# Early stage of a graph network kernel: centring of x shared by ScalarE and POOL, turning over two banks, and four smaller moves

## The reference

```python
h = relu(layernorm(x))
# self loops are added to edge_index once more inside; deg counts both
dinv = rsqrt(segment_sum(1, dst));  norm = dinv[src] * dinv[dst]
conv(h, W, b) = segment_sum((h @ W)[src] * norm, dst) + b
x1 = x + conv(relu(conv(relu(conv(h, W1, b1)), W2, b2)), W3, b3)
h = relu(layernorm(x1))
red = segment_sum(h[src] + relvectors[edge_type], dst)
out = x1 + gru_cell(red, h)
```

## Time and profile before

| | us |
|---|---|
| median of 3 runs (range) | 964.29 (962.75 to 965.47) |
| the profiled execution, whole | 963.61 |
| its span | 959.3 |
| PE busy | 913.2 (95%) |
| DVE busy | 480.2 (50%) |
| ACT busy | 291.5 (30%) |
| POOL busy | 18.7 (2%) |

### The profile page before, as it was taken

The page is one execution under the profiler, slowest core; times in us unless marked ns, Lnnn a source line. Parts: engine busy times, 40 slices in busy tenths (PEclk is TensorE's granted clock), DMA queues, the critical chain, the costliest instruction groups (busy, mean ns, idle before and its releaser), DMA issues.

```text
span 959.3 us, 15812 instructions
## 1 busy us (share of the span) xinstructions
PE 913.2 (95%) x6300; PEld 567.1 (59%) x6300; DVE 480.2 (50%) x1266; ACT 291.5 (30%) x569; POOL 18.7 (2%) x29
## 2 busy tenths in 40 slices
PE   2879999999999989999999999999999999999996
PEld 1358788888888875544445544444455455555553
DVE  7956889899988810211114233333535033333436
ACT  3565455555555520100112022111332121212222
POOL 0000100000000000000000000000000000000000
PEclk9979999999999999999999999999999999999999
DMA  6000000000000040000000011111321000100010
GB/s 210 5 1 1 3 12 18 13 13 13 13 13 13 13 160 1 2 1 1 0 1 11 29 34 44 39 34 39 97 74 30 8 22 23 33 23 22 23 33 30
DMA packets 27350, 27.65 MB, mean 29 GB/s; under 512 B 3217, under 2 KB 25901, under 8 KB 27272
## 3 DMA queue, kind: packets, MB, share of 16 engines
q1 hardware_dynamic: 26600, 26.18, 8.7%
q10 hardware_dynamic: 672, 0.41, 0.1%
HBM read 17.43 MB, written 9.15 MB: 28 GB/s over the span
## 4 chain that ended last, share of the span: by engine, by line
PE 91%; DVE 5%; ACT 2%; issue 1%; DMA 0%; SPq 0%; ACTq 0%; DVEq 0%
PE ps L1079 41%; PE ps L789 12%; PE ps L697 11%; PE ps L549 9%; PE ps L1090 5%; PE ps L553 5%; PE ps L1110 2%; PE ps L769 2%; DVE node_b L798 1%; PE ps L702 1%; PE ps L713 1%; PE ps L756 1%; PE ps L737 1%; PE ps L534 1%; PE ps L711 0%
## 5 line engine op out<-in xcount | busy, mean ns | idle before, releaser
L1079 PE MATMUL ps<-count,node_b 128*128 128x512 f16 (+3 forms) x1400 | 271.2, 352 | 0.4 <-DVE node_b L1241 0.3
L798 DVE TENSOR_TENSOR node_b<-node_b 128x50 f16<-128x50 f16 (+4 forms) x455 | 209.3, 526 | 10.6 <-PE ps L697 9.9
L1079 PEld LDWEIGHTS ps<-count,node_b 128*128 128x128 f16 (+2 forms) x1400 | 121.4, 97 | 142.4 <-issue 8.2
L697 PE MATMUL ps<-node_b 128*128 128x225 f16 (+1 forms) x808 | 165.8, 288 | 9.4 <-DVE node_b L798 9.4
L1000 ACT ACTIVATE count<-ps 128x500 f32 x202 | 122.8, 608 | 127.2 <-PE ps L697 120.9
L789 PE MATMUL ps<-node_a,count 128*128 128x256 f16 (+1 forms) x1050 | 149.1, 273 | 0.0
L1079 PE MATMUL ps<-count,node_a 128*128 128x512 f16 (+3 forms) x700 | 135.4, 352 | 0.0
L789 PEld LDWEIGHTS ps<-node_a,count 128*128 128x128 f16 (+1 forms) x1050 | 100.0, 98 | 21.6 <-issue 7.6
L1079 PEld LDWEIGHTS ps<-count,node_a 128*128 128x128 f16 (+1 forms) x700 | 60.0, 97 | 74.1 <-issue 7.2
L702 PE MATMUL ps<-node_b,params 128*128 128x9 f16 (+1 forms) x808 | 101.4, 174 | 0.0
L697 PEld LDWEIGHTS ps<-node_b 128*128 128x128 f16 x808 | 81.3, 101 | 17.8 <-DVE node_b L798 7.1
(11 more groups left out here) (196 smaller groups left out, 809.5 us busy)
## 6 DMA issues: line engine op xcount, KB each, us to landing
node_a<-in_x SPq DMA_DIRECT2D x4, 768.0 KB, 7.6
table_scratch<-agg SPq DMA_DIRECT2D x21, 128.0 KB, 1.7
node_b<-table_scratch SPq DMA_DIRECT2D x3, 768.0 KB, 6.8
xt<-x_scratch SPq DMA_DIRECT2D x16, 128.0 KB, 2.1
out<-scaled SPq DMA_DIRECT2D x16, 128.0 KB, 1.7
xt<-in_x SPq DMA_DIRECT2D x12, 128.0 KB, 2.1
params<-in_x SPq DMA_DIRECT2D x12, 128.0 KB, 2.0
x_scratch<-xt SPq DMA_DIRECT2D x12, 128.0 KB, 1.7
```

The source lines that it names most:

```text
L697: return PE.matmul(window(s)[:, :, first:first + n], low, key_hot[k][j // 2][:, j % 2, :, i].rearrange("p (t w) -> p t w", w=n), start=(s ...
L798: return DVE.tensor_tensor(to, iota, keys.unsqueeze(2).to_broadcast([P, n, width, 2]), ALU.is_equal)
L1079: last = PE.matmul(ps[:, b, 0:cols], nodes[0:k, t, part, f * P:(f + 1) * P], count[0:k, t, c * CHUNK:c * CHUNK + cols], start=(n == 0 and ...
```

## The change

- The root's table: ACT takes one small square root at the start of its program, ahead of the loads of the edge types.
- Centring: ACT centres the even tiles in their beats, POOL the odd ones at the start of `fast_pool`, as soon as the sums are there.
- Turning: tiles 0 to 8 use bank 6 as before; from tile 9 on, tiles alternate between banks 6 and 7, and PE waits for the relu of the tile before the last.
- Ranks' counts: both halves go into bank 5, as rows 0 to 19 and 32 to 51 of one sum; ACT copies them out in one instruction, and four matmuls turn them in place of eight. The moving operand of L737 is now pairs out of every four, and `both_ranks`, made by DVE in beat 0, adds the two sets of rows.
- `COLUMNS`: PE's beat 25 becomes beat 7; DVE's maximum moves from beat 33 to beat 16, and the steps for the scales become six.
- The end of the build: 24 of the 1050 early products are kept for the last block. What is left to do for tiles 19 and 20 on DVE and ACT comes behind the last loops and the last window; SP stores these two within the reload of the last group.

```diff
-        picks, counts_t = aside(4, 2 * WINDOW - 1), aside(5, EACH)
+
+        COUNT_ROWS = 32 + WINDOW
+        picks, counts_t = aside(4, 2 * COUNT_ROWS - 1), aside(5, EACH // 2).rearrange("p (s j) -> p s j", j=2)
+        both_ranks = aside(4, WINDOW, 2 * COUNT_ROWS)
...
+            ACTE.activation(scales[:, 7:8], asked[:, 0, 0:1], ACT.Sqrt).then_inc(*act_seq.up())
             load_rows(ACTE, rel_row, rel, types_in)
...
-        SCALE_STEPS = 7
+        SCALE_STEPS = 6
...
-        COLUMNS_AT = 25
+        COLUMNS_AT = 7
+        COLUMNS_OUT_AT = 16
+        LATER_TURNS = 8
...
-        products_after = [-(-max(s + 1 - PRODUCTS_FROM, 0) * len(early_products) // (NS - PRODUCTS_FROM)) for s in range(NS)]
-        assert products_after[-1] == len(early_products)
+
+        LAST_PRODUCTS = 24
+        products_after = [-(-max(s + 1 - PRODUCTS_FROM, 0) * (len(early_products) - LAST_PRODUCTS) // (NS - PRODUCTS_FROM)) for s in range(NS)]
+        products_after[-1] = len(early_products)
...
-        counts_bank = (5, 7)
-        CNT, HIST, TURNED = ps[:, 5, 0:WINDOW * Q], ps[:, 5, WINDOW * Q:WINDOW * Q + T], ps[:, 6, 0:D].rearrange("p (f n) -> p f n", f=HALVES)
+        RANKS = ps[0:COUNT_ROWS, 5, 0:EACH // 2].rearrange("p (s j) -> p s j", j=2)
+        CNT, HIST = ps[:, 5, 0:WINDOW * Q], ps[:, 5, WINDOW * Q:WINDOW * Q + T]
+
+        def turned(t):
+            bank = 6 if t <= LATER_TURNS else 6 + t % 2
+            return ps[:, bank, 0:D].rearrange("p (f n) -> p f n", f=HALVES)
...
                 PE.wait_ge(ranks_ready, beat + 2)
-                for h, bank in enumerate(counts_bank):
-                    last = PE.matmul(ps[0:WINDOW, bank, 0:EACH // 2], picks[:, WINDOW - 1 - beat:2 * WINDOW - 1 - beat],
-                                     rank_is[beat][:, h * EACH // 2:(h + 1) * EACH // 2], start=(beat == 0), stop=(beat == WINDOW - 1))
+                ranks = rank_is[beat].rearrange("p (s j) -> p s j", j=QUARTERS)
+                for h in range(2):
+                    row = 32 * h + beat
+                    last = PE.matmul(RANKS, picks[:, COUNT_ROWS - 1 - row:2 * COUNT_ROWS - 1 - row], ranks[:, :, 2 * h:2 * h + 2],
+                                     start=(beat == 0 and h == 0), stop=(beat == WINDOW - 1 and h == 1))
                 if beat == WINDOW - 1:
                     last.then_inc(ranks_counted, 1)
             if beat == COUNTS_AT:
-                PE.wait_ge(counts_out, 2)
+                PE.wait_ge(counts_out, 1)
                 for q in range(Q):
-                    for j in range(QUARTERS):
-                        last = PE.matmul(CNT[0:lanes(q), q * WINDOW:(q + 1) * WINDOW],
-                                         counts_t[0:WINDOW, :].rearrange("p (s j) -> p s j", j=QUARTERS)[:, q * P:q * P + lanes(q), j],
-                                         ident16[0:WINDOW, 0:WINDOW], start=(j == 0), stop=(j == QUARTERS - 1))
+                    for j in range(2):
+                        last = PE.matmul(CNT[0:lanes(q), q * WINDOW:(q + 1) * WINDOW], counts_t[0:COUNT_ROWS, q * P:q * P + lanes(q), j],
+                                         both_ranks[0:COUNT_ROWS, :], start=(j == 0), stop=(j == 1))
                 last.then_inc(counts_done, 1)
             t = beat - TURN_AT
             if 0 <= t < T:
                 m = rows(t)
-                PE.wait_ge(x_centred, t + 1)
+                PE.wait_ge(x_centred[t % 2], t // 2 + 1)
+                if t == LATER_TURNS + 1:
+                    PE.wait_ge(columns_read, 1)
                 if t:
-                    PE.wait_ge(x_turned_out, t)
+                    PE.wait_ge(x_turned_out, t if t <= LATER_TURNS else t - 1)
                 for f in range(HALVES):
-                    last = PE.transpose(TURNED[:, f, 0:m], h1[0:m, t, f * P:(f + 1) * P], ident[0:m, 0:m])
+                    last = PE.transpose(turned(t)[:, f, 0:m], h1[0:m, t, f * P:(f + 1) * P], ident[0:m, 0:m])
                 last.then_inc(x_turned, 1)
...
-                    PE.wait_ge(columns_read, 1)
...
             if beat == COLUMNS_AT:
                 PE.wait_ge(abs_made, 2)
-                PE.wait_ge(counts_out, 2)
...
-                        if s == min(summed_at[u] + OUT_AT, NS - 1):
+                        if s == summed_at[u] + OUT_AT:
                             out_bias_dve(u)
-                        if s == min(summed_at[u] + OUT_LOW_AT, NS - 1):
+                        if s == summed_at[u] + OUT_LOW_AT:
                             out_low_dve(u)
             DVE.wait_ge(win_written, NS)
             loops(ALU.add, EARLY).then_inc(chunk_looped, 1)
+            for u in range(EARLY):
+                if summed_at[u] + OUT_AT >= NS:
+                    out_bias_dve(u)
+                if summed_at[u] + OUT_LOW_AT >= NS:
+                    out_low_dve(u)
 
         def beside_dve(beat):
 
             if beat == 0:
                 DVE.memset(picks, 0.0).then_inc(*dve_seq.up())
                 DVE.wait_ge(*dve_seq.now)
-                DVE.memset(picks[:, WINDOW - 1:WINDOW], 1.0).then_inc(ranks_ready, 1)
+                DVE.tensor_tensor(both_ranks, ident16[:, 0:WINDOW], ident16[:, 32:32 + WINDOW], ALU.add).then_inc(*dve_seq.up())
...
+            if beat == COLUMNS_OUT_AT:
+                columns_max_dve()
...
+        def columns_max_dve():
+            DVE.wait_ge(abs_summed, 1)
+            DVE.tensor_reduce(fours[:, 0:2], COLUMNS, AX_X, ALU.max).then_inc(columns_read, 1)
...
             if step == 0:
-                DVE.wait_ge(abs_summed, 1)
-                DVE.tensor_reduce(fours[:, 0:2], COLUMNS, AX_X, ALU.max).then_inc(columns_read, 1)
-            elif step == 1:
...
-                    if s == min(summed_at[u] + OUT_AT, NS - 1):
+                    if s == summed_at[u] + OUT_AT:
                         out_shape_act(u)
+            for u in range(EARLY):
+                if summed_at[u] + OUT_AT >= NS:
+                    out_shape_act(u)
...
+            if 0 <= t < T and t % 2 == 0:
                 m = rows(t)
                 ACTE.wait_ge(x_summed, min(t // 6, XG) + 1)
-                ACTE.activation(h1[0:m, t, :], h1[0:m, t, :], ACT.Identity, bias=moments[0:m, t, 0:1], scale=2.0).then_inc(x_centred, 1)
+                ACTE.activation(h1[0:m, t, :], h1[0:m, t, :], ACT.Identity, bias=moments[0:m, t, 0:1], scale=2.0).then_inc(x_centred[0], 1)
             t = beat - TURN_AT
             if 0 <= t < T:
                 m = rows(t)
                 ACTE.wait_ge(x_turned, t + 1)
-                ACTE.activation(turned_x(t)[:, :, 0:m], TURNED[:, :, 0:m], ACT.Relu).then_inc(x_turned_out, 1)
+                ACTE.activation(turned_x(t)[:, :, 0:m], turned(t)[:, :, 0:m], ACT.Relu).then_inc(x_turned_out, 1)
             if beat == WINDOW - 2:
                 ACTE.wait_ge(ranks_counted, 1)
-                for h, bank in enumerate(counts_bank):
-                    ACTE.activation(counts_t[0:WINDOW, h * EACH // 2:(h + 1) * EACH // 2], ps[0:WINDOW, bank, 0:EACH // 2],
-                                    ACT.Copy).then_inc(counts_out, 1)
+                ACTE.activation(counts_t[0:COUNT_ROWS, :, :], RANKS, ACT.Copy).then_inc(counts_out, 1)
...
-            for u in range(EARLY):
+            def store(u):
                 SP.wait_ge(node_ready, u + 1)
                 SP.dma_start(early_dram(u, u + 1)[:, 0, :], staged[u % 2].rearrange("p a d -> p (a d)")).then_inc(early_stored[u % 2], 16)
+
+            stored = next(u for u in range(EARLY) if summed_at[u] + OUT_LOW_AT >= NS)
+            for u in range(stored):
+                store(u)
             SP.wait_ge(win_done, NS)
             SP.wait_ge(win_written, NS)
-            for k in range(2):
-                SP.wait_ge(early_stored[k], 16 * len(range(k, EARLY, 2)))
             for g, (first, end) in enumerate(RELOADS):
+                for u in range(stored, end):
+                    store(u)
+                stored = max(stored, end)
+                for k in range(2):
+                    SP.wait_ge(early_stored[k], 16 * len(range(k, end, 2)))
                 SP.dma_start(node_b[:, first:end, :, :].rearrange("p t a d -> p t (a d)"), early_dram(first, end)).then_inc(early_in[g], 16)
...
         def fast_pool():
+            for t in range(1, T, 2):
+                m = rows(t)
+                POOL.wait_ge(x_summed, min(t // 6, XG) + 1)
+                POOL.tensor_scalar(h1[0:m, t, :], h1[0:m, t, :], 2.0, moments[0:m, t, 0:1], ALU.mult, ALU.add).then_inc(x_centred[1], 1)
             POOL.wait_ge(small_maxed, 2)
......
```

More of the change, by code:

```diff
@@ L597, in program @@
         w_early_in, bias1_in, small_in = [sem(f"w_early_in{i}") for i in range(2)], sem("bias1_in"), sem("small_in")
-        x_centred, x_turned, x_turned_out, x_weighted = (sem(n) for n in ("x_centred", "x_turned", "x_turned_out", "x_weighted"))
+        x_turned, x_turned_out, x_weighted = (sem(n) for n in ("x_turned", "x_turned_out", "x_weighted"))
+        x_centred = [sem(f"x_centred{i}") for i in range(2)]
```

(15 more changed lines are left out.)

## The result

| | before | after |
|---|---|---|
| median, us (range) | 964.41 (962.75 to 965.47, 4 runs) | 955.34 (953.45 to 956.55, 4 runs) |
| the profiled execution, whole | 963.61 | 956.55 |
| its span | 959.3 | 952.4 |

The changed kernel takes 0.9906 of the time, 95% interval 0.9882 to 0.9929: 9.1 us less, where the forecast had 6.6. The profiled execution is the longest of the four.

What follows compares the result with a forecast made beforehand. PE was taken as the bound from 100 to 338 us, so gains could come only between 20 and 100 us and at the 338 us gap. 4.2 + 2.35 = 6.6 us off gave 957.7 us, range 953.5 to 964.0.

Steps and rivals of the forecast that it cites:

- (g): End of the build: 46 products behind the last window remove PE's 2.43 us wait before L1110, 2.35 net.
- Root's table: ACT's early table load delays the edge types' issue by 1.5 us against slack of 3.4: no effect.
- (a): DVE before window 2: 0.1 us for `both_ranks`, three collisions with POOL at 0.23 each; window 2 0.8 us later.
- (b): Columns' sums in PE's beat 7: 2.3 us, bounds 1.65 and 3.3; PE 3.1 us late by then.
- (c): Tiles 0 to 11: 0.5 us saved on tiles 9 to 11, another 0.7 in rounds; window 6 at 49.5.
- (d): Tiles 12 to 15: ACT sets the pace, 2.9 us; window 7 at 52.4, DVE begins L897 at 53.4.
- (e): From L897 to window 8: DVE needs 1.25 and 2.05 us; window 8 at 56.8, 3.5 us ahead.
- (f): Window 8 to the degrees: 0.7 us saved, bounds 0 and 1.5; 4.2 us ahead at the first early product.
- clock stays up: Rival: denser work keeps PE at 2.4 GHz up to 100 us, giving 955.0 us; chance 0.15.
- Port: Rival: DVE and POOL share their way to memory; 12 centrings cost DVE 10.1 us, giving 964.1; chance 0.18.
- Slow centring: Rival: POOL too slow for its 12 tiles; at 4 us each the kernel takes 973.3 us; chance 0.07.

Runs made afterwards that it cites:

- after_again: The changed kernel once more, nothing altered: 956.11 us, 0.9916 of the kernel before.
- front_only: The changed kernel without the part at the end of the build: 959.55 us, 0.9948 of the kernel before.
- cols_3_warm: Changed kernel with columns in beat 3, maxima in 10, two banks throughout, POOL centring odd tiles to 17, tiles 19 and 24's transposes repeated: 951.57 us.
- end_only: The kernel before with only the end's part, 24 early products kept for the last block: 961.63 us, 0.9971 of the kernel before.
- all_pool: The changed kernel with all 25 tiles centred by POOL, none by ACT: 955.07 us, 0.9902 of the kernel before.
- act_all: The changed kernel with all 25 tiles centred by ACT, none by POOL: 955.28 us, 0.9907 of the kernel before.

## Why the prediction was right

The measured 955.34 lies within the range of 953.5 to 964.0, 2.4 us below the forecast of 957.7: the steps are right, and their sum is too small. Its own steps against the profile after.

| step | forecast | profile after |
|---|---|---|
| window 6 | 49.5 | 49.87 |
| window 7 | 52.4 | 52.54 |
| DVE begins L897 (now L919) | 53.4 | 53.67 |
| window 8 | 56.8 | 57.06 |
| degrees' first scale step | 61.3 | 61.53 |
| window 10 | 64.3 | 64.28 |
| first early product | 96.4 | 97.13 |
| the end, (g) | 2.35 | 3.18 |

- *Root's table*, nothing: right. ACT issued its last load at 6.45 us instead of 6.11, not 1.5 late, because the issues ran on beside the load of the table; taken away, the load made no difference in time.
- *(a)*, 0.8: too dear. 0.56 in the profile, of which 0.40 is the start; the runs leave 0.15, DVE's beat 0. The three collisions of 0.23 did not happen: the centring stretches, the one-hots don't. The price came from POOL's addition, with two inputs, where the centring has one.
- *(b)*, 2.3: right for the columns, whose pitch is 2.26 us (34.82 to 37.08). But window 2 to window 3 took 6.30 in place of 3.05, 3.25 more: window 2's own work and the ranks behind it ran slower too, 1.22 in place of 0.75 and 2.89 in place of 2.37, at the lower clock. (b) priced the columns and put nothing for that. It differs from one execution to the next: in `after_again` the same way is 5.41, in `front_only` 6.70. PE is 3.81 late at window 3, where (a) and (b) had 3.1.
- *(c), (d)*: right. Window 3 to window 6 took 12.79 us in place of 14.37, 1.6 less (forecast 1.2); tiles 9 to 11 go at 0.83 (0.81). The strided operand costs nothing by the column: one rank matmul takes 0.34 as before. A pair takes 0.54 against 0.51; in tiles 9 to 11, where PE sets the pace, that is most of what they are above 0.81. Whether the step or the 52 output rows in place of 20 cause it was not tried. ACT's busy 4.76 of 5 us in the stretch of (d) is the bound that was named, and DVE's cover at L919 was 2.74, not 0.9, as its work there cost less than (a) had it.
- *(e), (f)*: right to 0.3 us, in part because errors met: PE was 0.7 later at window 3 than forecast, (c) gave 0.4 more than it had, and DVE's cover took up the rest. From window 10 to the first early product the forecast took "the same work", 32.04; it took 32.85, since weighing ran 5.30 us at a granted clock still low. From kernel to kernel that way lies between 31.52 (`cols_3_warm`) and 33.06 (`front_only`).
- *(g)*: the term that was mis-sized. The idle 2.43 went as forecast, and 0.75 more came out of the product phase. There the windows' blocks follow each other on PE at 1.2 or 1.3 us, and some at 0.2 more (1.4 or 1.5): 24 of these before, 21 after, which is 0.6 of the 0.75. The forecast put nothing for this, and the rows below show where it lies. Also, 29 products stand behind the last window (24 and the 5 of before), not the 46 that (g) had; it did no harm, as the loops' end at 331.97 still comes before PE's end at 333.98.

The longer blocks, PE's timeline of the kernel before:

```profile
133.57 0.28 PE L697 MATMUL ps<-node_b 128*128 128x225 f16 x1
...
134.32 0.93 PE L789 MATMUL ps<-node_a,count 53*128 53x256 f16 x6
135.09 0.27 PE L697 MATMUL ps<-node_b 128*128 128x225 f16 x1
```

The last source tile has 53 rows, so each destination tile ends with two products of 53 rows among all the others of 128. Each block of 1.4 or 1.5 us has one of these at its end, in its middle or, as here, at its start. Where the pair is divided between two blocks, both are longer. By `products_after` that happens four times before (at 149, 349, 799 and 999 products) and once after (999), and so with 20 such pairs ahead of the last block there are 24 and 21 long blocks. `front_only` has 24 too, `end_only` 21. The 0.6 us are thus a side effect of the new spread over the blocks, and luck as far as the change goes; 0.15 have no place.

The sum: 3.5 us at the first early product (forecast 4.2) and 3.2 behind (2.35), 6.7 of the span's 6.9. The timed gain is 2 us more than the profiled one, since a profile is a single execution. `after_again` is the same code, with a span of 951.1. Its stretches:

```profile
30.00:38.30 8.30, 7.16 (x41) 4.33 (x42) 8.30 (x27) 1.12 (x3) 4.05 (x5) 0.79 0.01 2
52.60:60.30 7.70, 5.24 (x76) 4.08 (x73) 4.90 (x16) 5.25 (x15) 0.39 (x1) 0.85 0.01 2
```

The granted clock is 0.79 and 0.85 here where the changed kernel's profile has 0.66 and 0.73, and with it 0.9 us are saved between windows 2 and 3 (5.41 against 6.30) and 0.7 between windows 8 and 10 (6.55 against 7.22). The kernel before varies likewise: from the start to the first early product it takes 81.7 us, the same code in `end_only` 83.1. The new front takes 77.8, and 76.1 and 78.5 in `after_again` and `front_only`. The means differ by 4.9 us, close to the timed 5.1 of `front_only`; so the 3.5 came from a pair of executions that shows less than most, and the 4.2 of step (f) was 0.9 too small by the timed runs. In which step that lies single profiles can't say.

The rival *clock stays up* is not what happened: a granted clock of 0.50 from 60.3 to 65 us, which is the lower level throughout, and of 0.92 behind it say so; `after_again` has 0.50 and 0.95.

*Port* is refuted by the one-hots' 2.13 and by `all_pool`, which doubles POOL's share and costs nothing. A few of DVE's small instructions do show the sharing: L457 and L459 take 0.28 and 0.42 with POOL beside them, 0.19 and 0.18 in `act_all`. They lay in DVE's cover. *Slow centring* is refuted too: twelve centrings have a median of 0.53 us and a longest of 2.58, and no turn waited for POOL.

## What to carry to other kernels

When two engines hand a tile back and forth through one buffer, read the period from the starts of equal rows and compare it with each engine's own work: the difference (here 0.97 against 0.83) is what a second buffer gives, and only while nothing else is queued. A piece of work that is free to move belongs where its engine waits, which is a row with an idle time of about the size of the piece; here that choice alone was worth 2.3 to 2.9 us, a quarter to a third of the change. Price the parts one by one: the second bank is worth 3.8 us and the end 3.0, while the root's table and the sharing between ACT and POOL, which gave the change its name, show nothing in time. The ranks' single sum was not taken out by itself. Where a wait is removed, look for who is second: the 2.6 us of waiting at L962 went into 2.7 at the degrees.
